# First tokens and taps loaded first, statistics ahead of the taps' product, and two steps of the step-size chain moved to VectorE

## The chip, the core and the metric

The kernel runs on one core of one Trainium2 chip. The core has five engines that take their instructions in order, each from its own list: TensorE (PE in the profile), VectorE (DVE), ScalarE (ACT), GpSimd (POOL) and SyncE (SP), which here issues the loads and stores. They meet only through semaphores. The metric is the device time of one execution, in microseconds, as the median of several.

## The reference, cut to what matters

Two layers, each a mixer and a feed-forward part, every part on a layer norm of the running sum, over 2048 tokens of 128 features. The change lies in the first part, a selective scan:

```python
xz = x @ in_proj_w                       # 128 -> 512, split into x_in and z
x_in, z = jnp.split(xz, 2, axis=-1)
xc = silu(causal_conv(x_in, conv_w, 4 taps) + conv_b)
ssm_out = xc @ x_proj_w                  # B (16), C (16) and one column for dt
dt = softplus(ssm_out[..., -1:] @ dt_w + dt_b)
A = -jnp.exp(A_log)
y = _selective_scan(xc, dt, A, B_p, C_p, D_param)
return y * silu(z) @ out_proj_w
```

The scan needs exp(dt * A) and dt * B * xc for 16 states of 256 channels. After it come a mixture of 8 experts and a shared one, an attention with 16 heads whose queries and keys pass convolutions, and a second mixture with a choice of 2 of 8 experts.

## The kernel before, in words

The tokens are taken in four chunks of 512. The scan part runs over `k` = 0 to 63, 16 states for each chunk, and each `k` has two halves `g` of 128 channels. `scan_order` (line 77) is an order written out by hand that each engine's program goes through with its own functions: first `start()`, then for each `k` the steps `rows`, `scanP`, `mulW`, `mulB`, `scanX`, `mulC`, `clamp` and `sums`, with the next chunk's `prolog` and the last chunk's `epilog` and feed-forward pulled in between piece by piece. `attention_order` is the like for what follows.

The change touches the start, chunk 0. SyncE issues all loads in one queue: `x_tok` (all 2048 tokens, 1 MB, semaphore `d_x`), then nine loads under one semaphore `d_scan`, the input projection `w_in` and the convolution's taps `w_cv` ahead of seven small ones down to `w_out`, then the feed-forward weights (`d_ffn`) and the attention's (`d_att`); after these it goes into `start()` (line 2169), where it writes the rows B and C to `bc` in HBM, and then issues the row loads of `rows(k)`.

VectorE multiplies the taps into `w_in` (line 1389), so that convolution and projection are one product on TensorE, copies `starts` into bank 2 of PSUM (line 1392), and takes the statistics of chunk 0 in `norm` (lines 1397 and 1401). GpSimd's `power` (from line 1879) makes the inverse deviation and the shift. ScalarE normalizes (line 1111), TensorE transposes (line 615), ScalarE copies back (line 1117), and TensorE does the tap products (line 626) into banks 7 and 6, the gate products (line 630) and, behind ScalarE's two Silus (line 1121), the row product (line 634) and the step-size products (line 638).

The step size is softplus(v) = max(v, 0) + log(1 + exp(-|v|)), the logarithm by three quartics: ScalarE does |v| (line 1132), the exponential (line 1134), the positive part (line 1135) into `vv2`, and pairs of squares (lines 1143 and 1147, the second written to the bank that held v); VectorE multiplies the three factors (line 1412) and adds the positive part (line 1417) to give `DL[0]`. GpSimd multiplies this with the convolved input `U[0]` into `DU[0]` (line 1906). ScalarE's `rows(0)` makes exp(dt * A) (line 1206), GpSimd's `clamp` (line 1942) bounds it, and `mulB` (line 1926) multiplies `DU` with B. Then VectorE's scans follow (lines 1449, 1455, 1463).

Of the kernel before, what the change touches and what calls it, by code (L numbers as in the profile page):

```python
# [6 lines left out]
ALU = mybir.AluOpType  # L7
ACT = mybir.ActivationFunctionType
# [58 lines left out]
def drain(gen):  # L67
    for _ in gen or ():
        pass
# [328 lines left out]
def build(nc, A, out):  # L398
    with ExitStack() as ctx:
        S = Signals(nc, ctx)  # L400
# [6 lines left out]
        def bank(i):  # L407
            return PS[:, i, :]

        x_tok = sb("x_tok", [128, NB, 128])  # L410
# [3 lines left out]
        cst = sb("cst", [128, 6])  # L414
# [32 lines left out]
        with ExitStack() as ph:  # L447
# [3 lines left out]
            w_in = D2[:, 6144:6656]  # L451
# [5 lines left out]
            w_db = sa("w_db", [128, 2])  # L457
# [114 lines left out]
            w.wait_ge(S("end"), 5)  # L572


        X_IN, W_SCAN, W_FFN, W_ATT = 16, 16 * 9, 16 * 12, 16 * 14
        KEY_ROWS = 16 * 18
        W_EXPERTS = 16 * 35

# [524 lines left out]
        def scalar_program(e):  # L1103
# [10 lines left out]
            def start():  # L1114
                scaled(0, 0, xn1, 0, "p")
                w.wait_ge(S("p_tp"), 1)
                e.activation(XN[:, 0:C], bank(7), ACT.Copy).then_inc(S("p_ln"), 1)
                w.wait_ge(S("d_scan"), W_SCAN)
                for g in range(2):
                    w.wait_ge(S("p_mm_x"), g + 1)  # L1120
# [9 lines left out]
                for g in range(2):  # L1130
                    w.wait_ge(S("p_mm_dt"), g + 1)
                    e.activation(yy2[g], bank(7 - g), ACT.Abs, bias=w_db[:, g:g + 1]).then_inc(S("s_abs"), 1)
                    w.wait_ge(S("s_abs"), g + 1)
                    e.activation(yy2[g], yy2[g], ACT.Exp, scale=-1.0).then_inc(S("s_exp"), 1)
                    e.activation(vv2[g], bank(7 - g), ACT.Relu, bias=w_db[:, g:g + 1]).then_inc(S("s_vv"), 1)
                for r in range(3):
                    for g in range(2):
                        n = 4 * r + 2 * g
# [245 lines left out]
        def vector_program(e):  # L1384
            w = Waits(e)
            e.memset(xnT[:, 0:1], 0.0).then_inc(S("edge"), 1)
            e.memset(xnT[:, T + 1:T + 2], 0.0).then_inc(S("edge"), 1)
            w.wait_ge(S("d_scan"), W_SCAN)
            e.tensor_tensor(w_cv[:, :, :], w_cv[:, :, :], w_in[:, 0:256].unsqueeze(1).to_broadcast([128, 4, 256]),
                            ALU.mult).then_inc(S("taps"), 1)  # L1390
            w.wait_ge(S("const"), 11)
            e.tensor_copy(bank(2), starts[:, :]).then_inc(S("starts"), 1)

            def norm(i, tc, st, pre, pause=2):

# [6 lines left out]
                yield from idle(pause + 2)  # L1402

            def start():
                w.wait_ge(S("d_x"), X_IN)
                drain(norm(0, 0, 0, "p"))
                for r, (_, _, more) in enumerate(QUARTICS):
                    for g in range(2):
                        if r:
                            w.wait_ge(S("s_pp"), 2 * r + g - 1)  # L1410
                        w.wait_ge(S("s_sq"), 4 * r + 2 * g + 2)
                        e.scalar_tensor_tensor(out=pp2[g], in0=bank(7 - g), scalar=more, in1=pp2[g] if r else yy2[g],
                                               op0=ALU.add, op1=ALU.mult).then_inc(S("s_pp"), 1)
                for g in range(2):
                    w.wait_ge(S("s_pp"), 5 + g)
                    w.wait_ge(S("s_vv"), g + 1)
                    e.scalar_tensor_tensor(out=DL[0][:, g, :], in0=pp2[g], scalar=LEAD, in1=vv2[g], op0=ALU.mult,
                                           op1=ALU.add).then_inc(S("p_dl"), 1)

            def prolog(tc):  # L1420
                Dx = DL[tc % 2]
                yield from norm(tc, tc, 4 * (tc % 2), "p")
                yield from idle(11)
                for g in range(2):
# [440 lines left out]
        def gpsimd_program(e):  # L1865
# [30 lines left out]
            def start():  # L1896
                power(0, 0, "p")
                for x in range(8):
                    e.memset(rank[:, :, x], 8.0 - x).then_inc(S("tables"), 1)
                w.wait_ge(S("d_scan"), W_SCAN)  # L1900
                for g in range(2):
                    e.tensor_scalar(skip[:, g, :], ident[:, :], w_D[:, g:g + 1], None, ALU.mult).then_inc(S("tables"), 1)
                for g in range(2):
                    w.wait_ge(S("p_dl"), g + 1)
                    w.wait_ge(S("p_u"), g + 1)
                    e.tensor_tensor(DU[0][:, g, :], DL[0][:, g, :], U[0][:, g, :], ALU.mult).then_inc(S("p_du"), 1)

            def prolog(tc):
                yield
                power(tc, 4 * (tc % 2), "p")  # L1910
# [220 lines left out]

        def sync_program(e):
            w = Waits(e)
            e.dma_start(x_tok[:, :, :], A["L0_attn_x"].rearrange("o (b p) d -> p (o b) d", p=128)).then_inc(S("d_x"), 16)
            e.dma_start(w_in[:, :], A["L0_attn_in_proj_w"]).then_inc(S("d_scan"), 16)
            e.dma_start(w_cv[:, :, :], A["conv_taps"].partition_broadcast(128)).then_inc(S("d_scan"), 16)
            e.dma_start(w_cb[:, :], A["L0_attn_conv_b"]).then_inc(S("d_scan"), 16)
            e.dma_start(w_xp[:, :, :], A["L0_attn_x_proj_w"].rearrange("(g p) n -> p g n", p=128)).then_inc(
                S("d_scan"), 16)
# [1 line left out]
            e.dma_start(w_db[:, :], A["L0_attn_dt_b"]).then_inc(S("d_scan"), 16)  # L2141
            e.dma_start(w_al[:, :, :], A["L0_attn_A_log"].rearrange("(g p) n -> p g n", p=128)).then_inc(
                S("d_scan"), 16)
            e.dma_start(w_D[:, :], A["L0_attn_D_param"]).then_inc(S("d_scan"), 16)
            e.dma_start(w_out[:, :, :], A["L0_attn_out_proj_w"].rearrange("(g p) n -> p g n", p=128)).then_inc(
                S("d_scan"), 16)
# [246 lines left out]
```

## Time and profile before

| what | value |
|---|---|
| times of three runs, us | 1527.34, 1530.22, 1535.51 (median 1530.22) |
| profiled execution: span of its instructions, us | 1529.1 |
| profiled execution: its own time | not listed apart from the three |
| busy share of the span | TensorE 85%, VectorE 79%, ScalarE 69%, GpSimd 44% |
| busy before 54 us | TensorE 15.43, VectorE 10.41, ScalarE 25.03, GpSimd 10.62 |
| mean granted TensorE clock, of full speed | 0.932 |

The profile is of one execution. Its starts are counted from the first instruction. "Idle before, releaser" is the time for which an engine had nothing to run ahead of a group, and what ended that. A line's number is that of the code above. The KB column of the DMA view shows 0.5 for `x_tok`, the size of one of its pieces; the whole is 1 MB.

### The profile page before, as it was taken

The numbers are of one execution on the slowest core, as the hardware profiler recorded it, in microseconds if no ns is written. First come the engines' busy times: TensorE is split into PE (matmuls) and PEld (weight loads), VectorE is DVE, ScalarE is ACT, GpSimd is POOL, SyncE is SP. The second block draws the span as 40 slices with busy tenths as digits, with TensorE's granted clock in tenths as the row PEclk, the third lists the DMA queues.
The fourth block names the chain that finished last, engine by engine and source line by source line (L and its number), as shares of the span: only waits on it lengthen the run. The fifth ranks groups of instructions, "written<-read, shape, count | busy, mean of one in ns | idle before, by whom it ended". The sixth has DMA issues, their size and how long they took to land.

```text
span 1529.1 us, 22573 instructions
## 1 busy us (share of the span) xinstructions
PE 1305.2 (85%) x8424; PEld 506.3 (33%) x8424; DVE 1206.0 (79%) x1435; ACT 1058.4 (69%) x1839; POOL 668.8 (44%) x652
## 2 busy tenths in 40 slices
PE   4364689988977997886499999999999998999998
PEld 1121234333443443332122222222222222236963
DVE  0799988898989871776699999999999997933522
ACT  3552379768837825453179998999899987997643
POOL 1688868977978856661403112111111123111430
PEclk9677789999988998997689999999999998999999
DMA  8221222223323202421213001100010000010210
GB/s 220 66 82 70 76 66 88 90 70 83 96 70 84 82 21 55 88 43 37 41 35 51 30 30 48 23 2 2 2 23 2 2 2 19 6 29 12 74 32 28
DMA packets 63696, 75.71 MB, mean 50 GB/s; under 512 B 8633, under 2 KB 39226, under 8 KB 63458
## 3 DMA queue, kind: packets, MB, share of 16 engines
q1 hardware_dynamic: 62818, 72.70, 17.9%
q0 software_dynamic: 768, 1.57, 0.3%
q8 instruction: 66, 1.08, 0.3%
q14 instruction: 44, 0.36, 0.1%
HBM read 66.04 MB, written 8.21 MB: 49 GB/s over the span
## 4 chain that ended last, share of the span: by engine, by line
PE 52%; DVE 26%; ACT 9%; issue 7%; POOL 4%; DMA 1%; SPq 1%; another core or an unknown queue 0%; DVEq 0%; POOLq 0%; ACTq 0%
DVE mx L1670 16%; PE PS L980 11%; PE PS L968 6%; PE PS L736 5%; PE PS L745 5%; PE PS L937 4%; PE PS L688 2%; PE PS L1052 2%; PE PS L1067 2%; DVE D L1463 2%; DVE PS L1449 2%; PE PS L1088 2%; PE PS L1076 2%; ACT D L1206 1%; POOL D L1926 1%
## 5 line engine op out<-in xcount | busy, mean ns | idle before, releaser
L1343 ACT ACTIVATE aa<-PS 128x512 f32<-128x512 f32 x1024 | 551.7, 598 | 63.0 <-PE PS L968 51.4
L1670 DVE TENSOR_REDUCE mx<-PS 128x2 f32<-128x1024 f32 x480 | 552.8, 1215 | 15.6 <-PE PS L937 7.3
L980 PE MATMUL PS<-aa,D 128*32 128x256 f32 x4096 | 322.9, 393 | 1.5 <-ACT aa L1343 0.6
L968 PE MATMUL PS<-D 54*128 54x512 bf16 x1024 | 213.1, 391 | 13.0 <-ACT aa L1343 8.3
L2044 POOL CAST n<-nm 4x512 bf16<-4x512 f32 x15 | 9.0, 602 | 453.7 <-ACT nm L1325 453.7
L937 PE MATMUL PS<-D 51*128 51x512 bf16 x960 | 191.3, 386 | 17.2 <-DVE mx L1670 16.6
L1449 DVE TENSOR_TENSOR_SCAN PS<-PS,D 128x512 f32<-128x512 f32 x128 | 157.5, 1231 | 11.1 <-POOL D L1942 3.5
L745 PE MATMUL PS<-xnT,f_w 128*128 128x512 f32 x288 | 158.3, 644 | 6.1 <-ACT HB L1233 5.5
L1233 ACT ACTIVATE HB<-PS 128x512 f32<-128x512 f32 x144 | 84.1, 595 | 104.7 <-PE PS L745 98.4
L736 PE MATMUL PS<-HB,f_w 128*128 128x512 f32 x288 | 146.3, 618 | 6.1 <-DVE GO L1537 5.9
L980 PEld LDWEIGHTS PS<-aa,D 128*32 128x32 f32 x4096 | 84.3, 108 | 192.8 <-issue 154.3
L1206 ACT ACTIVATE D<-D,Am 128x512 f32<-128x512 f32 x128 | 85.1, 713 | 75.7 <-DVE D L1463 73.7
L688 PE MATMUL PS<-D,ident 128*128 128x512 f32 x192 | 107.5, 685 | 32.9 <-POOL D L1933 28.1
L1933 POOL TENSOR_TENSOR D<-D 128x1024 f32<-128x1024 f32 x48 | 112.9, 2353 | 48.5 <-DVE D L1463 48.3
L968 PEld LDWEIGHTS PS<-D 54*128 54x128 bf16 x1024 | 53.4, 93 | 225.3 <-ACT aa L1343 160.1
L1463 DVE TENSOR_TENSOR_SCAN D<-D,hl,PS 128x512 f32<-128x512 f32 x96 | 122.6, 1277 | 2.9
L1926 POOL TENSOR_TENSOR D<-D 128x1024 f32<-128x1024 f32 x48 | 112.8, 2350 | 3.3
L736 PEld LDWEIGHTS PS<-HB,f_w 128*128 128x128 f32 x288 | 57.0, 200 | 82.8 <-issue 70.5
L745 PEld LDWEIGHTS PS<-xnT,f_w 128*128 128x128 f32 x288 | 53.9, 200 | 73.3 <-issue 51.6
L688 PEld LDWEIGHTS PS<-D,ident 128*128 128x128 f32 x192 | 39.4, 213 | 90.6 <-issue 50.9
L1455 DVE SCALAR_TENSOR_TENSOR PS<-PS,D 128x512 f32<-128x512 f32 x96 | 66.8, 696 | 2.8 <-POOL D L1926 0.5
L1942 POOL TENSOR_SCALAR D<-D 128x1024 f32<-128x1024 f32 x64 | 66.5, 1040 | 5.5
(333 smaller groups left out, 1700.2 us busy)
## 6 DMA issues: line engine op xcount, KB each, us to landing
D<-bc SPq DMA_DIRECT2D x128, 256.0 KB, 3.5
GB<-gd SPq DMA_DIRECT2D x32, 256.0 KB, 3.7
D<-sc SPq DMA_DIRECT2D x72, 64.0 KB
aa<-in_L_ffn_W SPq DMA_DIRECT2D x9, 256.0 KB, 3.2
D<-in_L_ffn_W SPq DMA_DIRECT2D x9, 256.0 KB, 3.6
f_w<-in_L_ffn_experts_w SPq DMA_DIRECT2D x1, 2048.0 KB, 9.2
f_w<-in_L_ffn_experts_w SPq DMA_DIRECT2D x8, 256.0 KB, 5.9
aa<-gh SPq DMA_DIRECT2D x1, 2048.0 KB, 8.3
```

The source lines that it names most:

```text
L688: e.matmul(bank(g), ident[:, :], wb[k % 4][:, g, :], start=(n == 0), stop=(n == 15)).then_inc(S("mm_sum"), 1)
L736: e.matmul(down_bank(tc, n // 4), f_w2[:, n // 4, n % 4, :], HB1[i % 6], start=(n % 4 == 0), stop=(n % 4 == 3)).then_inc(S("mm_down"), 1)
L745: e.matmul(bank(4 + i % 2), f_w1[:, n // 4, 128 * (n % 4):128 * (n % 4) + 128], XN[:, ts], start=True, stop=True).then_inc(S("mm_up"), 1)
L937: t = e.matmul(to[:, hh, :], query(hh, qc % 2, p, b), KS[64 * hh:64 * hh + 51, p, 512 * c:512 * c + 512], start=True, stop=True)
L968: e.matmul(take_exp(s + hh), KS[64 * hh:64 * hh + 54, p, 128 * kb:128 * kb + 128], QP[64 * hh:64 * hh + 54, qc % 2, p, :], start=True, sto ...
L980: t = e.matmul(PS[32 * j:32 * j + 32, 7, cs], va[:, kb, 9 * h:9 * h + 32], Pt[K % 3][:, 512 * j + 256 * n:512 * j + 256 * n + 256], start= ...
L1343: e.activation(Pt[K % 3][:, c:c + 512], bank((s + hh) % 3), ACT.Exp).then_inc(S("e_free"), 1)
L1449: e.tensor_tensor_scan(out=bank(3), data0=bank(2), data1=ab[k % 3][:, g, :], initial=0.0, op0=ALU.max, op1=ALU.mult).then_inc(S("sP"), 1)
L1463: e.tensor_tensor_scan(out=pb[k % 2][:, g, :], data0=ab[k % 3][:, g, :], data1=bank(3), initial=hl[:, 16 * g + n:16 * g + n + 1] if tc els ...
L1670: e.tensor_reduce(mx4[:, G % 2, b, 2 * pair:2 * pair + 2, c:c + 1], max_banks(m), AX.X, ALU.max).then_inc(freed(m)[0], 1)
L1926: e.tensor_tensor(wb[k % 4], DU[tc % 2][:, :, :], Bb[k % 3].unsqueeze(1).to_broadcast([128, 2, C]), ALU.mult).then_inc(S("wB"), 1)
L1933: e.tensor_tensor(wb[k % 4], pb[k % 2], Cb[k % 3].unsqueeze(1).to_broadcast([128, 2, C]), ALU.mult).then_inc(S("xC"), 1)
```

## The change

Five edits, all at the start of the kernel.

1. SyncE loads the first four of the 16 token blocks first (256 KB, semaphore `d_x0`), then `w_in` and the taps under a semaphore of their own (`d_taps`), then five small loads, then the other twelve token blocks (`d_x`), then `w_D` and `w_out`. `d_scan` now counts seven loads. VectorE's `prolog` waits for `d_x` before its statistics.
2. VectorE takes the statistics of chunk 0 first, and multiplies the taps and copies `starts` after them.
3. ScalarE runs one Silu over one column of constants, into a place of `Am` that is written again later, after it has copied the transposed tokens back.
4. The positive part of chunk 0 is one VectorE instruction for each half, add and then maximum, and waits for ScalarE's |v| of that half.
5. `DU[0]` is made by VectorE, after `DL[0]`, and no longer by GpSimd.

```diff
@@ -572,7 +572,7 @@
             w.wait_ge(S("end"), 5)
 
 
-        X_IN, W_SCAN, W_FFN, W_ATT = 16, 16 * 9, 16 * 12, 16 * 14
+        X_IN, W_TAPS, W_SCAN, W_FFN, W_ATT = 16, 16 * 2, 16 * 7, 16 * 12, 16 * 14
         KEY_ROWS = 16 * 18
         W_EXPERTS = 16 * 35
 
@@ -1115,6 +1115,8 @@
                 scaled(0, 0, xn1, 0, "p")
                 w.wait_ge(S("p_tp"), 1)
                 e.activation(XN[:, 0:C], bank(7), ACT.Copy).then_inc(S("p_ln"), 1)
+                w.wait_ge(S("const"), 8)
+                e.activation(Am[:, 0:1], cst[:, 0:1], ACT.Silu)
                 w.wait_ge(S("d_scan"), W_SCAN)
                 for g in range(2):
                     w.wait_ge(S("p_mm_x"), g + 1)
@@ -1132,7 +1134,6 @@
                     e.activation(yy2[g], bank(7 - g), ACT.Abs, bias=w_db[:, g:g + 1]).then_inc(S("s_abs"), 1)
                     w.wait_ge(S("s_abs"), g + 1)
                     e.activation(yy2[g], yy2[g], ACT.Exp, scale=-1.0).then_inc(S("s_exp"), 1)
-                    e.activation(vv2[g], bank(7 - g), ACT.Relu, bias=w_db[:, g:g + 1]).then_inc(S("s_vv"), 1)
                 for r in range(3):
                     for g in range(2):
                         n = 4 * r + 2 * g
@@ -1385,11 +1386,6 @@
             w = Waits(e)
             e.memset(xnT[:, 0:1], 0.0).then_inc(S("edge"), 1)
             e.memset(xnT[:, T + 1:T + 2], 0.0).then_inc(S("edge"), 1)
-            w.wait_ge(S("d_scan"), W_SCAN)
-            e.tensor_tensor(w_cv[:, :, :], w_cv[:, :, :], w_in[:, 0:256].unsqueeze(1).to_broadcast([128, 4, 256]),
-                            ALU.mult).then_inc(S("taps"), 1)
-            w.wait_ge(S("const"), 11)
-            e.tensor_copy(bank(2), starts[:, :]).then_inc(S("starts"), 1)
 
             def norm(i, tc, st, pre, pause=2):
 
@@ -1402,8 +1398,17 @@
                 yield from idle(pause + 2)
 
             def start():
-                w.wait_ge(S("d_x"), X_IN)
+                w.wait_ge(S("d_x0"), X_IN)
                 drain(norm(0, 0, 0, "p"))
+                w.wait_ge(S("d_taps"), W_TAPS)
+                e.tensor_tensor(w_cv[:, :, :], w_cv[:, :, :], w_in[:, 0:256].unsqueeze(1).to_broadcast([128, 4, 256]),
+                                ALU.mult).then_inc(S("taps"), 1)
+                w.wait_ge(S("const"), 11)
+                e.tensor_copy(bank(2), starts[:, :]).then_inc(S("starts"), 1)
+                w.wait_ge(S("d_scan"), W_SCAN)
+                for g in range(2):
+                    w.wait_ge(S("s_abs"), g + 1)
+                    e.tensor_scalar(vv2[g], bank(7 - g), w_db[:, g:g + 1], 0.0, ALU.add, ALU.max).then_inc(S("s_vv"), 1)
                 for r, (_, _, more) in enumerate(QUARTICS):
                     for g in range(2):
                         if r:
@@ -1416,9 +1421,14 @@
                     w.wait_ge(S("s_vv"), g + 1)
                     e.scalar_tensor_tensor(out=DL[0][:, g, :], in0=pp2[g], scalar=LEAD, in1=vv2[g], op0=ALU.mult,
                                            op1=ALU.add).then_inc(S("p_dl"), 1)
+                for g in range(2):
+                    w.wait_ge(S("p_dl"), g + 1)
+                    w.wait_ge(S("p_u"), g + 1)
+                    e.tensor_tensor(DU[0][:, g, :], DL[0][:, g, :], U[0][:, g, :], ALU.mult).then_inc(S("p_du"), 1)
 
             def prolog(tc):
                 Dx = DL[tc % 2]
+                w.wait_ge(S("d_x"), X_IN)
                 yield from norm(tc, tc, 4 * (tc % 2), "p")
                 yield from idle(11)
                 for g in range(2):
@@ -1900,11 +1910,6 @@
                 w.wait_ge(S("d_scan"), W_SCAN)
                 for g in range(2):
                     e.tensor_scalar(skip[:, g, :], ident[:, :], w_D[:, g:g + 1], None, ALU.mult).then_inc(S("tables"), 1)
-                for g in range(2):
-                    w.wait_ge(S("p_dl"), g + 1)
-                    w.wait_ge(S("p_u"), g + 1)
-                    e.tensor_tensor(DU[0][:, g, :], DL[0][:, g, :], U[0][:, g, :], ALU.mult).then_inc(S("p_du"), 1)
-
             def prolog(tc):
                 yield
                 power(tc, 4 * (tc % 2), "p")
@@ -2131,9 +2136,10 @@
 
         def sync_program(e):
             w = Waits(e)
-            e.dma_start(x_tok[:, :, :], A["L0_attn_x"].rearrange("o (b p) d -> p (o b) d", p=128)).then_inc(S("d_x"), 16)
-            e.dma_start(w_in[:, :], A["L0_attn_in_proj_w"]).then_inc(S("d_scan"), 16)
-            e.dma_start(w_cv[:, :, :], A["conv_taps"].partition_broadcast(128)).then_inc(S("d_scan"), 16)
+            tokens = A["L0_attn_x"].rearrange("o (b p) d -> p (o b) d", p=128)
+            e.dma_start(x_tok[:, 0:4, :], tokens[:, 0:4, :]).then_inc(S("d_x0"), 16)
+            e.dma_start(w_in[:, :], A["L0_attn_in_proj_w"]).then_inc(S("d_taps"), 16)
+            e.dma_start(w_cv[:, :, :], A["conv_taps"].partition_broadcast(128)).then_inc(S("d_taps"), 16)
             e.dma_start(w_cb[:, :], A["L0_attn_conv_b"]).then_inc(S("d_scan"), 16)
             e.dma_start(w_xp[:, :, :], A["L0_attn_x_proj_w"].rearrange("(g p) n -> p g n", p=128)).then_inc(
                 S("d_scan"), 16)
@@ -2141,6 +2147,7 @@
             e.dma_start(w_db[:, :], A["L0_attn_dt_b"]).then_inc(S("d_scan"), 16)
             e.dma_start(w_al[:, :, :], A["L0_attn_A_log"].rearrange("(g p) n -> p g n", p=128)).then_inc(
                 S("d_scan"), 16)
+            e.dma_start(x_tok[:, 4:16, :], tokens[:, 4:16, :]).then_inc(S("d_x"), 16)
             e.dma_start(w_D[:, :], A["L0_attn_D_param"]).then_inc(S("d_scan"), 16)
             e.dma_start(w_out[:, :, :], A["L0_attn_out_proj_w"].rearrange("(g p) n -> p g n", p=128)).then_inc(
                 S("d_scan"), 16)
```

## Rows read from the trace of the kernel before

**Rows 1.** The chain that ended last: shares of the span by engine (page).

```profile
PE 52%; DVE 26%; ACT 9%; issue 7%; POOL 4%; DMA 1%; SPq 1%; another core or an unknown queue 0%; DVEq 0%; POOLq 0%; ACTq 0%
```

**Rows 2.** Windows; columns: TensorE, weight load, VectorE, ScalarE, GpSimd, granted clock, DMA share, GB/s.

```profile
0.00:54.00 54.00, 15.43 (x32) 6.10 (x32) 10.41 (x25) 25.03 (x39) 10.62 (x33) 0.84 0.63 178
54.00:86.00 32.00, 20.44 (x43) 8.13 (x44) 30.37 (x33) 15.88 (x23) 28.84 (x23) 0.79 0.16 52
...
162.00:1000.00 838.00, 723.04 (x3620) 276.70 (x3620) 704.38 (x872) 568.96 (x886) 467.19 (x446) 0.93 0.23 59
```

**Rows 3.** Waits, 0 to 45 us: total, times, longest.

```profile
DVE D L1389 <- DMA w_out<-in_L_attn_out_proj_w: 10.1, 1, 10.1
```

**Rows 4.** Timeline, 0 to 20 us; columns: start, us, engine, line, what.

```profile
0.86 0.88 SPq L2134 DMA_DIRECT2D x_tok<-in_L_attn_x  x1
...
11.08 1.23 DVE L1389 TENSOR_TENSOR D<-D 128x1024 f32<-128x1024 f32 x1 [10.11 <-DMA w_out<-in_L_attn_out_proj_w]
...
12.81 0.86 DVE L1397 BATCH_NORM_STATS2 st<-x_tok 128x6 f32<-128x128 f32 x4
...
19.85 8.81 PE L626 MATMUL PS<-xnT,D 128*128 128x512 f32 x16 [0.78 <-ACT xnT L1117]
```

**Rows 5.** DMA issues, of the start and then whole span: KB, us to landing.

```profile
x_tok<-in_L_attn_x SPq DMA_DIRECT2D x1, 0.5 KB, 6.5
...
D<-bc SPq DMA_DIRECT2D x128, 256.0 KB, 3.5
```

**Rows 6.** Line 2183 (row loads of B), 30 to 60 us.

```profile
L2183 SPq DMA_DIRECT2D D<-bc x4: 320/381/433, 34.5 to 54.4; - x4
...
DMA to landing us min/median/max: 3.4/4.6/5.5
```

**Rows 7.** Timeline, weight loads of the tap passes.

```profile
22.55 0.34 PEld L626 LDWEIGHTS PS<-xnT,D 128*128 128x128 f32 x1 [0.52 <-issue]
...
23.37 0.19 PEld L626 LDWEIGHTS PS<-xnT,D 128*128 128x128 f32 x1 [0.48 <-issue]
23.80 0.19 PEld L626 LDWEIGHTS PS<-xnT,D 128*128 128x128 f32 x1 [0.24 <-issue]
```

**Rows 8.** Timeline of ScalarE, 25 to 39 us.

```profile
25.32 1.28 ACT L1121 ACT_TABLE_LOAD   x1 [5.62 <-PE PS L626]
...
28.70 0.69 ACT L1121 ACTIVATE U<-PS,w_cb 128x512 f32<-128x512 f32 x1 [1.39 <-PE PS L626]
...
35.78 0.67 ACT L1135 ACTIVATE D<-PS,w_db 128x512 f32<-128x512 f32 x1
36.35 0.68 ACT L1132 ACTIVATE GO<-PS,w_db 128x512 f32<-128x512 f32 x1
...
37.60 0.67 ACT L1135 ACTIVATE FO<-PS,w_db 128x512 f32<-128x512 f32 x1
38.17 0.71 ACT L1143 ACTIVATE SQ<-D,cst 128x512 f32<-128x512 f32 x1
```

**Rows 9.** Timeline, 28 to 52 us (a narrower window gives fewer of a group).

```profile
28.65 0.44 SPq L2167 DMA_DIRECT2D bb<-in_L_attn_out_b  x1
...
32.87 0.33 SPq L2171 DMA_DIRECT2D bc<-D  x1
...
47.74 0.68 DVE L1417 SCALAR_TENSOR_TENSOR D<-GO,FO 128x512 f32<-128x512 f32 x1
47.91 2.86 POOL L1906 TENSOR_TENSOR D<-D,U 128x512 f32<-128x512 f32 x2 [30.32 <-DVE D L1417]
...
47.91 1.64 POOL L1906 TENSOR_TENSOR D<-D,U 128x512 f32<-128x512 f32 x1 [30.32 <-DVE D L1417]
47.92 1.95 ACT L1206 ACTIVATE D<-D,Am 128x512 f32<-128x512 f32 x3 [1.49 <-DVE D L1417]
...
50.86 1.04 POOL L1942 TENSOR_SCALAR D<-D 128x1024 f32<-128x1024 f32 x1
```

**Rows 10.** VectorE's groups by line and form: busy us, mean ns.

```profile
L1854 DVE TENSOR_TENSOR aa<-aa 128x512 f32<-128x512 f32 x7 | 4.8, 691 | 0.2
```

## What the change does to the time: the prediction

> **What bounds the kernel now.** I read the chain that ended last first: its largest shares are TensorE (52%) and VectorE (26%) [rows 1]. Those are averages over stages with different limits, so next come the windows by stage [rows 2]. The reader is to see that in the first 54 us no engine is busy for half of the time: this stretch is a string of waits, one engine at a time. From 54 to 86 us VectorE is busy 30.4 of 32 us and GpSimd 28.8, and from 162 to 1000 us TensorE and VectorE share the load at a granted clock of 0.93. The change touches only the first 54 us. Everything behind it depends on what the start hands over (the first step sizes), nothing behind it waits for a fixed hour, and so whatever is taken off this string should arrive at the end, if the later stages run as before.
>
> The string, step by step. VectorE does nothing until 11.08, and the wait view names the last of the nine loads that it counts, the one of w_out [rows 3]. Then it multiplies the taps (1.23 us), copies `starts`, and only at 12.81 begins the statistics of the first tokens, whose load had landed 6.5 us after its issue at 0.86, at 7.4 [rows 4, 5]. From the statistics over GpSimd's power, ScalarE's normalization, transposes and copy to the first tap product on TensorE (19.85) it is 7.04 us [rows 4]. Then come products and activations, the quartics' squares from 38.17 [rows 8], the second step size at 47.74, GpSimd's two products of step size and input, its clamp at 50.86, and the scan [rows 9].
>
> **The start of the loads and the order on VectorE.** This is the largest term. Statistics now wait for 256 KB of tokens alone. The trace has no such load at the start; the nearest row is a load of the same 256 KB over a quiet queue, 3.5 us at the median [rows 5]. From above the bound is the 6.5 us that the 1 MB took, from below the 3.4 us of the fastest row load of that size in the start [rows 6]. I take 3.5, because the size is the same and the queue empty: the tokens are there at 0.86 + 3.5 = 4.36. Nothing stands ahead of the statistics on VectorE now but two tiny memsets. With the 7.04 us of before, the tap products could begin at 4.36 + 7.04 = 11.40 instead of 19.85: **8.45 us earlier**.
>
> They also need the taps' product. Its two loads (256 and 512 KB) stand behind the 256 KB of tokens, together the 1 MB that x_tok was before, so I expect them at about 7.4; three issues instead of one cost the queue some tenths (0.88 us for the large one [rows 4]), and their packets are no smaller. The product then ends at 7.4 + 1.23 = 8.6, well ahead of 11.40, and the copy of `starts` behind it too (it is wanted only by the scan). If the taps came as late as the last load does now, the product would end at 12.3 and the gain would be 7.5 instead of 8.45. The remaining 12 of the 16 token blocks land near 9 to 10 us; their reader is the next prolog, which begins its statistics only after 52 us, so the new wait for `d_x` there is free. The seven loads left under `d_scan` stay ahead of the large weights and land near 11 us as now, plus at most one issue; their first reader is the first Silu, at about 25.3 - 8.45 = 16.9. GpSimd's two `skip` products behind the same wait are done long before its clamp.
>
> SyncE's queue is what could spoil this, since a later step of the start issues from it. The write of the B and C rows waits for ScalarE's copy, and goes out at 32.87 now; SyncE is done with the weights at 28.65 + 0.44 = 29.1 [rows 9]. Shifted by 8.45 the copy would be ready at 24.4, so now the write waits for the queue until 29.1 and gains only 3.8 us. But its reader is not near: row loads land 3.4 to 5.5 us after their issue, which is 34.5 for the first [rows 6]. Even if it landed as late as today, at 40.0 at most, the first product that reads it would be wanted near 41. The queue hides this, with 1 us to spare in the worst case and 5 us in the likely one.
>
> **The Silu that loads its table early.** The table load of 1.28 us stands between the first tap product and the first Silu [rows 8]. It moves beside the tap products, at no cost, as ScalarE is idle there for 5.62 us [rows 8]. I count **no gain** for it: the second Silu waits again for TensorE, 1.39 us [rows 8], and TensorE works without a break through the gate products to the row product, which wants both. Bounds: 0 to 1.3 us.
>
> **The positive part on VectorE.** ScalarE loses two Relus, each 0.57 us from its start to the next instruction's (35.78 to 36.35 for the first, and the second stands likewise ahead of the square at 38.17) [rows 8]: 2 x 0.57 = **1.14 us**, on the path, since ScalarE has no idle time between them and the square. On VectorE, idle there, each costs some 0.69 us, between the end of the Abs that it now waits for and the first square written to the same bank; the tighter one starts at the second Abs's end and has two squares of slack. Without that cover it would cost up to 0.69. Queued behind its wait are only VectorE's quartic steps, which come after these squares anyway.
>
> **The first product of step size and input on VectorE.** GpSimd needs 2.86 us for the two, and its clamp waits for that until 50.86 [rows 9]. On VectorE a product of this form takes 0.691 us [rows 10]; behind the second step size (ends at 48.42) the two end near 49.7. The clamp then needs only ScalarE's two first decays: three take 1.95 us from 47.92, so two are there at about 49.25. Gain 50.86 - 49.25 = 1.6. But GpSimd's first product took 1.64 us while VectorE's last step size (two inputs in SBUF) ran beside it, the second 2.86 - 1.64 = 1.22 alone [rows 9]: 0.4 us of hindrance. The clamp would begin under VectorE's second product, which also reads two SBUF tensors, and I charge it the same 0.4: **1.2 us**, bounds 0.8 and 1.6. From there VectorE's scans follow as before. The Trainium skill ("GPSIMD Engine Reference", its table of the engine) says the same of this edit, and it speaks against it: GpSimd's SBUF interface is shared with VectorE and contended by VectorE instructions that read two SBUF inputs. Without the rule the sum would have 1.6 here, by it no more than 1.2; the trace agrees with it, by those 0.4 us. The taps' product can now run beside GpSimd's small power steps (5.8 to 7.9); the same effect could hold them for up to 1.2 us. I take nothing, as the taps land about when the last of them runs, and keep it in the range.
>
> **Sum.** 8.45 + 0 + 1.14 + 1.2 = 10.8 us. The profiled execution had a span of 1529.1 us, 1.1 below the median of the times (1530.2), and that I take for what lies around it. Span after: 1518.3. Time after: **1519.4 us**, 0.7% less.
>
> **The rivals.** (1) *The first tokens do not land first.* Packets of the three first loads share 16 engines; if they interleave, the tokens land only when the whole 1 MB has, at 7.4. For it: the 1 MB itself took 6.5 us. Against it: loads of 256 KB issued close together, the row loads of the start, still landed in 3.4 to 5.5 us [rows 6], and the tokens are issued first. Products at 7.4 + 7.04 = 14.4, first term 5.4 instead of 8.45, time 1522.4. Chance 12%.
>
> (2) *TensorE starts cold and stays so for longer.* The weight loads of the first tap passes come 0.82 us apart, from 23.37 on 0.43 [rows 7]: the engine went from its 1.2 GHz level to its 2.4 GHz level after the transposes and some four tap passes from 19.85 on, though the profile's column says 1.00 for this stretch. 28 passes lie on the path up to the step-size product, and about four were slow. If half of the other 24 stay slow in the new place (a pause before the taps would do that), that is 12 x 0.43 = 5 us: time 1524.4; if all do, 1529.7. Against it: the string of transposes, copy and products keeps its spacing. Chance 10%.
>
> (3) *The later stages run at a lower clock; this ends slower.* From 162 to 1000 us the mean clock is 0.93 [rows 2], so 2 x 0.07 x 838 = 117 us are already at 1.2 GHz, in a stretch where TensorE is busy 86% of the time. A start that comes 11 us sooner changes when its pauses fall. From the point where 22 us more are at half rate (a mean of 0.917), the gain of 10.8 is gone; at a mean of 0.90 it is 50 us more and up to 25 us lost, 1544 us. For it: nothing but this dependence on timing, and the three times of before, which differ by 8 us without any change. Against it: engines stay in step by the same waits, so the same pauses should recur. Chance 10%, half of it above 1538. The Trainium skill ("TensorE: Matmul & The Clock Gate", Part 1) calls the point at which the clock rises variable from run to run; no row here shows two runs of this.
>
> **How the numbers follow.** Forecast 68%, rivals 12, 10 and 10. The likeliest case's own range is 1515 to 1523: 1.6 us below for a faster load and no hindrance, and some 3 us of scatter on either side. The range that should hold 8 in 10 reaches down to 1513 and up to 1526, which takes in rival 1 and the half of rival 2, and leaves out the rest and rival 3. This kernel's measurement tells 0.5% (7.6 us) from no change, so faster means under 1522.6. Of the forecast's 68, 64 are below that, of rival 1's 12 half, of rivals 2 and 3 one each: 72% faster. Slower: 5%. The same: 23%.
>
> **What would show it.** Right: statistics of the first tokens begin at 4 to 5 us, ahead of the taps' product; first tap pass at 11 to 12; Silu's table load inside the tap products, with the gate products' end 8 to 9 us sooner; four ScalarE instructions between the last table load's users and the first square instead of six; clamp at 40 to 40.5 (50.86 - 10.8), near 1.1 us long or longer; first scan near 41. The stage windows behind it, moved by 11 us, should show the same busy times and the clock of 0.93. Wrong: statistics after 7 us (rival 1), more than six tap passes at 0.85 us (rival 2), a clock under 0.92 between 150 and 990 us (rival 3), or a first row load that lands after the clamp and holds the product.

## The result and the profile after

| | us |
|---|---|
| changed kernel, four runs | 1520.36, 1521.57, 1522.66, 1524.80 (median 1522.12) |
| kernel before, four runs | 1527.34, 1530.22, 1534.88, 1535.51 (median 1532.55) |
| ratio | 0.994, 95% interval 0.9924 to 0.9956 |
| profiled execution: time, span, mean granted clock | 1522.66, 1520.9, 0.921 |

The change takes 0.6% off, with 0.4 to 0.8% as the interval: the kernel is faster, and only the lower end of the interval is under the 0.5% that the prediction asked for. The forecast was 1519.4 with 1513 to 1526 as the range. Between medians the gain is 10.4 us where 10.8 were forecast; between the two profiled spans it is only 8.2.

First the start of the timeline, for the order of the loads and of VectorE (columns: start, us, engine, line, what).

```profile
0.80 0.43 SPq L2140 DMA_DIRECT2D x_tok<-in_L_attn_x  x1
...
3.69 0.87 DVE L1393 BATCH_NORM_STATS2 st<-x_tok 128x6 f32<-128x128 f32 x4 [2.73 <-DMA x_tok<-in_L_attn_x]
...
6.84 0.20 POOL L1903 TENSOR_TENSOR shift<-shift,rstd 128x4 f32<-128x4 f32 x1
...
7.37 1.23 DVE L1404 TENSOR_TENSOR D<-D 128x1024 f32<-128x1024 f32 x1 [2.39 <-DMA D<-in_conv_taps]
...
10.61 1.28 ACT L1119 ACT_TABLE_LOAD   x1
...
10.74 9.27 PE L626 MATMUL PS<-xnT,D 128*128 128x512 f32 x16 [0.78 <-ACT xnT L1117]
...
20.05 0.69 ACT L1123 ACTIVATE U<-PS,w_cb 128x512 f32<-128x512 f32 x1 [2.67 <-PE PS L626]
```

Statistics begin at 3.69 (12.81 before), the taps' product at 7.37, the first tap pass at 10.74 (19.85) [rows 4]. From statistics to tap pass it is 7.05 us, 7.04 before. Next the end of the start, for the three moved operations.

```profile
26.69 0.75 DVE L1411 TENSOR_SCALAR D<-PS,w_db 128x512 f32<-128x512 f32 x1 [17.49 <-ACT D L1134]
...
27.84 0.75 DVE L1411 TENSOR_SCALAR FO<-PS,w_db 128x512 f32<-128x512 f32 x1 [0.40 <-ACT GO L1134]
...
28.37 0.70 ACT L1144 ACTIVATE SQ<-D,cst 128x512 f32<-128x512 f32 x1
...
30.12 0.43 SPq L2178 DMA_DIRECT2D bc<-D  x1
...
33.34 0.32 SPq L2190 DMA_DIRECT2D D<-bc  x1
...
37.94 0.69 DVE L1422 SCALAR_TENSOR_TENSOR D<-GO,FO 128x512 f32<-128x512 f32 x1
...
38.54 1.29 DVE L1427 TENSOR_TENSOR D<-D,U 128x512 f32<-128x512 f32 x2
39.54 1.19 POOL L1947 TENSOR_SCALAR D<-D 128x1024 f32<-128x1024 f32 x1 [26.62 <-ACT D L1207]
40.76 1.23 DVE L1459 TENSOR_TENSOR_SCAN PS<-PS,D 128x512 f32<-128x512 f32 x1 [0.93 <-POOL D L1947]
```

The first square starts 9.80 us sooner than before, the second step size 9.80, the clamp 11.32 [rows 8, 9], and the first scan 11.18 (it began at 51.94). So the start gave more than the sum said. By the end of the span 8.2 are left. The stage windows do not show where the rest goes: from 162 us on TensorE and VectorE are busy for the same time as before within 0.4% [rows 2], ScalarE for 1% more and GpSimd for 2% less, at a clock of 0.92 and not 0.93.

```profile
0.00:54.00 54.00, 17.64 (x37) 7.47 (x38) 23.58 (x44) 28.23 (x46) 18.44 (x41) 0.77 0.67 191
...
162.00:1000.00 838.00, 725.86 (x3680) 276.71 (x3684) 703.55 (x865) 574.61 (x898) 458.44 (x438) 0.92 0.22 58
```

I laid the starts of VectorE's 128 scans of the first kind (those of line 1449 before, 1459 after) side by side. The changed kernel leads by 11.18 us at the first, by 9.75 from the thirteenth on (94.89 against 85.14), by 10.60 at the 67th, by 5.02 at the 83rd, and by 6.65 at the last (550.64 against 543.99). A new wait would take its share once and keep it; here the lead falls and rises again. The first fall can be read off one wait. VectorE stood idle for ScalarE's first square of the second chunk for 1.6 us before and for 3.0 us now, because the tap products that this square waits for took longer. Both kernels' rows, before:

```profile
64.53 5.26 PE L654 MATMUL PS<-xnT,D 128*128 128x512 f32 x8 [0.69 <-ACT xnT L1156]
```

and after:

```profile
53.36 6.74 PE L654 MATMUL PS<-xnT,D 128*128 128x512 f32 x8 [0.69 <-ACT xnT L1157]
```

The same eight passes, no wait among them: 6.74 us is eight at the half rate, 5.26 is about four at half and four at full rate (the eight passes of this line that follow, all at the full rate, take 3.60 in both). The largest fall, 2.8 us between the 71st and the 72nd scan, can be read off as well:

```profile
313.73 0.69 DVE L1490 TENSOR_TENSOR x_tok<-x_tok,PS 128x512 f32<-128x512 f32 x1 [2.70 <-PE PS L701]
```

VectorE waited 2.70 us for TensorE's products of line 701. Eight tap passes ahead of them (line 654) had taken 5.85 us; the kernel before does them in 3.70 and has no such wait.

### The profile page after: what moved, and what is told of

Read it like the earlier page. It is cut to its first block, busy times and chain, and to the rows that moved or that the text cites. A ratio compares the mean times of both kernels' runs of the same rounds, so it can differ in the third digit from the quotient of the medians.

```text
span 1520.9 us, 22574 instructions
## 1 busy us (share of the span) xinstructions
PE 1308.2 (86%) x8424; PEld 506.1 (33%) x8424; DVE 1210.3 (80%) x1439; ACT 1057.7 (70%) x1838; POOL 665.7 (44%) x650
## 4 chain that ended last, share of the span: by engine, by line
PE 50%; DVE 23%; POOL 9%; issue 8%; ACT 8%; DMA 2%; SPq 1%; another core or an unknown queue 0%; POOLq 0%; DVEq 0%; ACTq 0%
DVE mx L1680 15%; PE PS L980 12%; PE PS L968 6%; PE PS L745 5%; PE PS L736 5%; PE PS L937 4%; POOL D L1931 3%; PE PS L1052 2%; PE PS L1067 2%; PE PS L688 2%; PE PS L1088 2%; PE PS L1076 2%; POOL D L1947 2%; DVE D L1473 1%; PE PS L654 1%
```

## The experiments

**Theory A:** the start gives what its parts say, it arrives at the end in full, and what varies is how long TensorE runs at its 1.2 GHz level in the later stages. **Theory B:** the change brings in a new wait behind the first scan.

**The changed kernel once more, twelve runs.** No edit.

> The changed kernel once more, for its scatter. Theory A (the start gave 11 us, and up to 3 of them go lost or not by TensorE's clock in the scan and feed-forward stages): the first scan begins again at 40.8 us within 0.1, while the span differs from run to run by some us, and the runs with the higher mean clock are the shorter ones; about 1.5 to 2.5 us of span for 0.005 of clock. Theory B (the loss behind the first scan is a new wait that the change brings in, a row load or a full engine): every run ends 1520 to 1521, with no relation to the clock, and the shift against before falls at the same places.

Measured: median 1520.32 against 1529.59, ratio 0.995 (0.9934 to 0.9966). The first scan is at 41.26, and not within 0.1 of 40.8: the 16 tap passes took 9.77 us this time and not 9.27. The twelve runs fall into two groups: six with a mean clock of 0.930 or 0.931 have spans of 1515.5 to 1518.2 (mean 1516.7), six with 0.916 to 0.922 have 1519.0 to 1525.0 (mean 1522.6). The kernel before, on the same chip, had 0.926 to 0.933 in all of its 18 runs, and 1526.9 as the mean of the 13 at 0.929 or more. Between the runs of 0.929 and more the gain is 1526.9 - 1516.7 = 10.2 us.

The profile of this run is one of the first group: span 1516.2, clock 0.931. Set beside the kernel before (1529.1, 0.932), its scans lead by 10.68 us at the first and by 10.57 at the 128th, and by 10.57 to 10.70 everywhere between. The same program in the first profile led by 4.92 to 11.18. Theory B falls: a new wait of the program would be in both. VectorE's addition to `x_tok` of above, which waited 2.70 us for line 701, waits for nothing here, and the eight tap passes ahead took 3.70 us:

```profile
310.04 0.67 DVE L1490 TENSOR_TENSOR x_tok<-x_tok,PS 128x512 f32<-128x512 f32 x1
```

The windows of the two profiles of one and the same program, the longer one first:

```profile
86.00:151.00 65.00, 34.16 (x38) 10.74 (x39) 62.66 (x65) 17.84 (x27) 57.73 (x41) 0.53 0.22 73
...
300.00:450.00 150.00, 133.12 (x347) 60.86 (x345) 132.27 (x163) 103.04 (x137) 117.32 (x84) 0.91 0.26 75
```

```profile
86.00:151.00 65.00, 34.79 (x39) 11.17 (x40) 62.70 (x64) 16.89 (x26) 57.65 (x42) 0.68 0.24 75
...
300.00:450.00 150.00, 130.70 (x345) 60.50 (x343) 135.84 (x176) 101.65 (x136) 120.07 (x86) 0.94 0.25 78
```

From 86 to 151 us the clock 0.53 instead of 0.68 costs nothing (VectorE is busy 62.7 of 65 us in both). From 300 to 450 us 0.91 instead of 0.94 does: TensorE is busy longer, and VectorE gets less done.

**The loads and VectorE's order alone.** The kernel before with the first two of the five edits. Their main lines, cut (the taps' own semaphore, the second load of tokens and the copy of `starts` are as in the change):

```diff
-            e.dma_start(x_tok[:, :, :], ...).then_inc(S("d_x"), 16)
+            e.dma_start(x_tok[:, 0:4, :], tokens[:, 0:4, :]).then_inc(S("d_x0"), 16)
...
+                w.wait_ge(S("d_x0"), X_IN)
+                drain(norm(0, 0, 0, "p"))
+                w.wait_ge(S("d_taps"), W_TAPS)
+                e.tensor_tensor(w_cv[:, :, :], ...).then_inc(S("taps"), 1)
```

> The kernel before plus the loads' order, the split of x_tok and the order on VectorE; the early Silu, the Relus and the first product of step size and input as before. By the sum: first tap pass at 10.74 as in the changed kernel, first scan 8.65 sooner than 51.94, at 43.3; the time 8.7 us under before if all of it arrives at the end, 6 to 11 with the clock's scatter. A rival in which the other three edits carry the gain has the first scan at 48 or later.

Measured: 1519.5 against 1529.59, ratio 0.9932 (0.991 to 0.9955); first scan at 44.96, not 43.3. One us of the difference is a thing that I had named and taken at nothing. Its rows:

```profile
6.80 1.22 DVE L1403 TENSOR_TENSOR D<-D 128x1024 f32<-128x1024 f32 x1 [1.83 <-DMA D<-in_conv_taps]
6.84 1.25 POOL L1894 TENSOR_TENSOR shift<-shift,rstd 128x4 f32<-128x4 f32 x1
```

The taps landed at 6.80. GpSimd's last step, four numbers for each partition, then takes 1.25 us where it took 0.20 in the changed kernel's profile: it ends when VectorE's product of two SBUF tensors ends. ScalarE's normalization starts at 8.12, not 7.08. The other 0.6 us are TensorE's: the tap products took 9.90 us here, 9.27 there. The loads and the order carry most of the gain, 7.0 of 11.2 us at the first scan; in the time the other three edits made no difference that these runs can tell.

**VectorE's order undone.** The changed kernel, with the taps' product and the copy of `starts` put back ahead of the statistics.

> The changed kernel with the order on VectorE alone undone: the taps' product and the copy of starts stand ahead of the first statistics, the loads stay as changed. By the sum: statistics begin when the taps have landed (6.8 to 7.4) plus 1.8 us, near 9.0 instead of 3.7, so the first scan comes 5.2 us later, at 46 to 46.5, and the time 5 us over the changed kernel's. If only the loads' order mattered, the first scan would stay at 41 to 42.

Measured: 1519.88 against 1522.84, ratio 0.9978 (0.9965 to 0.9991). This is another chip, on which the changed kernel itself was not run, so its time can be set beside this one only by the ratios (0.995 on the first chip, 0.28% less, some 4 us; 5 were expected). Statistics at 8.26 and not 3.69, first tap pass at 15.30, 4.56 us later; first scan at 44.64, 3.9 us later only, because TensorE happened to be quicker (tap products in 8.59 us). That is less than the 5.2 us expected for the scan. The taps' product could start at 6.52 here, sooner than I had reckoned. The loads without the order bring the first tap pass from 19.85 to 15.30, half of the 9.1 us.

**The first load whole.** The changed kernel, with all 16 token blocks loaded first (and so without the `prolog`'s wait for `d_x`).

```diff
-            e.dma_start(x_tok[:, 0:4, :], tokens[:, 0:4, :]).then_inc(S("d_x0"), 16)
+            e.dma_start(x_tok[:, :, :], tokens).then_inc(S("d_x0"), 16)
...
-            e.dma_start(x_tok[:, 4:16, :], tokens[:, 4:16, :]).then_inc(S("d_x"), 16)
```

> The changed kernel with all 16 token blocks in the first load, as before, and all else as changed. By the sum: the 1 MB lands at 7.4, so statistics begin then and not at 3.7, and the taps, 768 KB behind it, near 9.5 to 10, with the product done by 11.3; first tap pass at 7.4 + 7.05 = 14.45, 3.7 us after that of the changed kernel, first scan at 44.5 to 45. If the order of the loads carried nothing, first scan at 41.

Measured: 1524.41 against 1529.76, ratio 0.9959 (0.9939 to 0.9979). Statistics at 7.28, the taps' product at 9.51, first tap pass at 14.48, first scan at 43.80. The first three are as expected; the scan came a little sooner, as the tap products took 8.57 us. GpSimd's last step was held again: it began at 10.43, inside VectorE's product (9.51 to 10.73), and took 0.36 us. The step ahead of it had begun at 9.31, before that product, and took its usual 1.04 us. The order without the split brings the first tap pass to 14.48, 5.4 of the 9.1 us; splitting the load adds the last 3.7. In this run and in the one before, the taps keep a semaphore of their own; that part of the change was not tested alone. An estimate from these rows: with the 1 MB load first the taps' product can start at 9.51, and statistics behind it begin 1.74 us later (6.52 to 8.26 in the run before this one), which makes 11.25 where the kernel before has 12.81: some 1.6 us.

**The early Silu undone.**

```diff
-                w.wait_ge(S("const"), 8)
-                e.activation(Am[:, 0:1], cst[:, 0:1], ACT.Silu)
```

> The changed kernel without the early Silu: the table load goes back between the first tap product and the first Silu. By the prediction nothing changes behind the second Silu, which again waits for TensorE: first scan 40.8 to 41.3, as in the changed kernel. A rival in which the load was on the path has the first scan 1.3 us later, at 42.1 to 42.6.

Measured: 1514.17 against 1522.84, ratio 0.9944 (0.9931 to 0.9957); first scan at 41.06. ScalarE's rows:

```profile
16.97 1.28 ACT L1121 ACT_TABLE_LOAD   x1 [6.53 <-PE PS L626]
18.27 0.69 ACT L1121 ACTIVATE U<-PS,w_cb 128x512 f32<-128x512 f32 x1
20.35 0.69 ACT L1121 ACTIVATE U<-PS,w_cb 128x512 f32<-128x512 f32 x1 [1.39 <-PE PS L626]
```

The table load is back in front of the first Silu, and the second waits for TensorE all the same, 1.39 us (2.67 with the early load). Worth nothing, as forecast.

**The positive part back on ScalarE.** The Relu of line 1135 back, VectorE's add and maximum out.

> The changed kernel with the positive part back on ScalarE. By the sum the first square starts 1.15 us later after the first |v|, 3.62 and not 2.47, and the first scan with it, near 42. Theory A on the clock (the start's phase decides how many tap and up products meet the lower clock) says that this small shift may also change how often runs fall near a clock of 0.92: 6 of 12 for the changed kernel, 0 of 18 for the one before. Theory B (an instruction of the change causes the low clock) says it stays at about half.

Measured: 1516.96 against 1522.84, ratio 0.9961 (0.9946 to 0.9976). The times of this kernel do not tell 1.1 us apart, but the profile does: from the first |v| (25.48) to the first square (29.10) 3.62 us, 2.47 in the changed kernel (25.90 to 28.37).

**The product of step size and input back on GpSimd.** Lines 1903 to 1906 back, VectorE's out.

> The changed kernel with the first product of step size and input back on GpSimd. By the sum the clamp waits for it, and the first scan comes 11.18 - 8.65 - 1.15 = 1.4 us later against the second step size (4.20 us after its start and not 2.82), at 42.2. On the clock as in the run with the positive part back on ScalarE: if a shift of the start by 1.4 us changes how often the clock is near 0.92, it is the phase and not an instruction.

Measured: 1518.65 against 1522.84, ratio 0.9969 (0.9957 to 0.9981). From the second step size to the first scan 4.20 us (37.52 to 41.72), 2.82 in the changed kernel: 1.38 us. The clamp's 1.04 us are 1.19 in the changed kernel, where it begins beside VectorE's second product: held by 0.15.

**Constant products on TensorE, ahead of the first transposes only, and ahead of the second chunk's too.** Nobody reads their results; the second kernel has both edits, the first only the first.

```diff
+                w.wait_ge(S("const"), 11)
+                for _ in range(4):
+                    e.matmul(bank(0), ident[:, :], starts[:, :], start=True, stop=True)
...
+                if tc == 1:
+                    w.wait_ge(S("p_st"), 16)
+                    for _ in range(6):
+                        e.matmul(bank(4), ident[:, :], starts[:, :], start=True, stop=True)
```

> The changed kernel plus the four products of constants ahead of the first transposes alone. Theory A: first scan at 38.7 (5 passes by 0.43 us), second chunk's first tap passes still slow, 5.3 to 6.8 us, as TensorE again idles for 25 us before them; time 2 us under the changed kernel, within its scatter. Theory B: the same start, and the same places of loss behind it.

> The changed kernel plus products of constants on TensorE whose results nobody reads: four ahead of the first transposes and six ahead of the second chunk's transposes, where it stands idle for 7 and 25 us. Theory A: the five tap passes of the start that were 0.85 us apart run at 0.43, first scan 2 us sooner (38.7), and the second chunk's first eight tap passes take 3.6 us and not 6.7, so the wait of VectorE for the second chunk's first square (3.0 us) goes away; together 3 to 5 us less than the changed kernel, about 1517.5. Theory B: the start gains 2 us, but nothing is gained at the second chunk. Against both: the products delay the transposes, no gain.

Measured: 1517.47 and 1517.38, beside 1520.32 for the changed kernel and 1529.59 for the one before, ratios 0.9935 (0.9915 to 0.9956) and 0.9928 (0.9906 to 0.995). First scans at 38.06 and 38.07. TensorE's rows of the kernel with both:

```profile
2.50 5.51 PE L621 MATMUL PS<-starts,ident 128*128 128x512 f32 x8 [2.50 <-POOL starts L1893]
8.79 0.66 PE L615 MATMUL PS<-ident,xn 128*128 128x128 f32 x4 [0.78 <-ACT xn L1117]
10.23 7.08 PE L628 MATMUL PS<-xnT,D 128*128 128x512 f32 x16 [0.78 <-ACT xnT L1123]
...
50.88 3.70 PE L660 MATMUL PS<-xnT,D 128*128 128x512 f32 x8 [0.69 <-ACT xnT L1163]
```

The 16 tap passes take 7.08 us instead of 9.27, and the second chunk's eight 3.70 instead of 6.74 (5.28 with the first edit alone). VectorE's wait for the second chunk's first square falls from 3.0 us to 0.2. So it was the clock: four products of constants ahead of the transposes change nothing else that these passes need. That the second edit then does not show in the time is within the scatter of five and six runs.

**Both, and the taps' product kept off GpSimd's last step.**

```diff
                 w.wait_ge(S("d_taps"), W_TAPS)
+                w.wait_ge(S("p_shift"), 1)
```

> The changed kernel with both sets of constant products on TensorE (as in the earlier run with both) and one more wait: the taps' product starts only after GpSimd's last step for the shift. In the run with the loads alone this step took 1.25 us instead of 0.20 because the taps had landed 0.04 us before it began; with the wait ScalarE's normalization starts at 6.8 to 7.1 in every run, and the taps' product, wanted at 10.2, ends at 8.4. First scan 38.0; time 10 to 14 us under the kernel before and 2 to 4 under the changed one, runs within 5 us of each other but for the clock.

Measured: 1518.5 against 1529.76, ratio 0.9924 (0.9906 to 0.9943), 11.3 us under the kernel before. First scan at 38.09, GpSimd's step 0.20 us. The added wait is not what did that here: the taps landed at 7.20, after the step had ended (6.99), so the wait held nothing and stays untested. The kernel beats the one before clearly. Against the changed kernel it leads by 2.7 us in the first scan; their ratios' intervals (0.9924 here, 0.995 and 0.994 there) overlap a little, and so do its runs (clocks 0.920 to 0.935): two of the six fell to 0.923 or less.

**The kernel before, with its start put off.** Four and five more copies of `starts` on VectorE ahead of the statistics, and nothing of the change.

> The kernel before, with four more copies of starts one after the other on VectorE, which only put off the first statistics, by 4 x 0.7 = 2.8 us. Theory A (where the start ends decides how often the clock of the later stages is near 0.92): the first scan is at 54.7, which lies against the start of the changed kernel as another place against TensorE's clock does; some runs of this kernel, perhaps half, then show a clock of 0.925 or less, and are 5 to 6 us longer than the others, though no instruction of the change is in it. Theory B (the change's own instructions do it): all runs stay at 0.929 to 0.934 like those of the kernel before, and the time is 2.8 us over it.

> The kernel before with five such copies, first scan 3.5 us later. Theory A: the share of runs with a clock of 0.925 or less differs from that of the run with four copies, and may be none at all. Theory B: none, time 3.5 us over the kernel before. If both delayed kernels never show the lower clock, the place of the start does not explain it and its cause stays open.

Measured: 1533.7 and 1534.8 against 1529.76, ratios 1.0026 (1.0012 to 1.004) and 1.0034 (1.002 to 1.0047), first scans at 55.22 and 55.49. A start that ends 3.3 and 3.6 us later ends the kernel 3.9 and 5.0 us later: what the start takes does arrive. On how often the clock is at 0.925 or less they say little: one run of 12, three of 12, and three of 26 of the kernel before beside them. Theory A had half of the runs with four copies. Over all runs the share was 3 of 62 for the kernel before, 9 of 16 for the changed one, 7 of 12 without the order, 4 of 9 with the whole load, 3 of 6 without the early Silu, 2 of 6 with the Relus back, 0 of 6 with GpSimd's product back, 0 of 4 with the loads alone, 6 of 17 for the three with constant products. The change makes it more frequent; what in it does is open.

The mark of 0.925 misses part of it. The scans of all the profiles, laid beside those of the kernel before like the first ones, show the lead in us (a minus is a lag):

| profile | clock | first scan | 83rd | 128th |
|---|---|---|---|---|
| changed kernel, once more | 0.931 | 10.68 | 10.60 | 10.57 |
| without the early Silu | 0.934 | 10.88 | 10.86 | 10.84 |
| constant products at the start | 0.931 | 13.88 | 13.82 | 13.80 |
| both constant products and the wait | 0.933 | 13.85 | 15.23 | 15.08 |
| changed kernel, first profile | 0.921 | 11.18 | 5.02 | 6.65 |
| both constant products | 0.924 | 13.87 | 10.57 | 12.20 |
| loads and order alone | 0.928 | 6.98 | 3.69 | 5.29 |
| without the order | 0.924 | 7.30 | 1.73 | 1.59 |
| the whole load | 0.921 | 8.14 | 2.56 | 2.43 |
| Relus back | 0.925 | 10.45 | 5.39 | 5.31 |
| GpSimd's product back | 0.926 | 10.22 | 5.44 | 5.41 |
| four copies more | 0.926 | -3.28 | -3.64 | -3.76 |
| five copies more | 0.925 | -3.55 | -9.38 | -7.77 |

Of the eleven profiles with an earlier start four kept their lead, seven lost part of it, among them the two whose shares are 0 of 6 and 0 of 4. So those shares acquit none of the edits. The kernel before with five copies lost 6 us in the same place without any instruction of the change. And the losses come in patterns that repeat: from the thirteenth scan on, the first profile of the changed kernel and that of the kernel with both constant products are 5.51 to 5.56 us apart at every scan, though one has the lower clock's long passes in the second chunk and the other does not; the changed kernel's second profile is 10.57 to 10.70 us from the kernel before. Which pattern an execution takes is not settled by the program alone: the changed kernel had both.

## Why the prediction was right, and where it was not

- **The largest term.** Forecast 8.45 us, from tokens landing 3.5 us after their issue. They took 2.9 (issue at 0.80, statistics at 3.69), so the first tap pass came 9.11 us sooner, of which TensorE gave back 0.46, its tap products taking 9.27 us and not 8.81. Mis-sized by 0.2 in sum; the 7.04 us from statistics to tap pass (7.05), and the taps at 7.4 (7.37), were right. The term holds by 8.65 us at the end of the tap passes. Rival 1, tokens no sooner than the rest, did not happen.
- **The table load.** Forecast nothing, shown to be nothing by undoing it.
- **The positive part.** 1.14 forecast, 1.15 measured (3.62 to 2.47), shown by undoing it. VectorE's 0.75 us lies in the cover, as said.
- **The first product on VectorE.** 1.2 forecast, 1.38 measured. The hindrance was there and smaller, 0.15 us and not 0.4, as the overlap was shorter. The Trainium skill's rule ("GPSIMD Engine Reference", table of the engine), that GpSimd's SBUF interface is contended by VectorE instructions with two SBUF inputs, agrees: 0.15 us at the clamp, 1.05 at the last step for the shift, each begun while such a VectorE instruction ran.
- **What I took at nothing there** was not always nothing. "As the taps land about when the last of them runs" was true, and which comes first changed: at 7.37 they were late enough, at 6.80 they cost 1.05 us, which I had bounded at 1.2.
- **SyncE's queue.** The write of the rows went out at 30.12, 29.1 forecast, as the queue was done with the weights only at 30.07, and then took 3.2 us instead of 1.6, so the first row load was issued at 33.34. With the longest landing of the first three B loads (6.1 us) it is there at 39.4, ahead of the first product at 40.81: it hid the loss, but with 1.4 us to spare and not the 5 that I called likely.
- **The sum.** 10.8 forecast up to the clamp and the scan, 11.2 measured; at the end 10.2 between the runs of 0.929 and more, 10.4 between the first medians, 9.3 between the medians of the 12 and 18 later runs. That 10.4 lies so near 10.8 is in part luck: three of the changed kernel's first four runs had a clock of 0.925 or less, and the kernel before had its highest median of all in its first four. The gain arrives in full where the later stages keep the pattern of the kernel before (10.68 us at the first scan and 10.57 at the last of the first kind); in other executions 2 to 6 us of it go lost by then. The forecast's "if the later stages run as before" was the condition that mattered. The 1.1 us taken for what lies around the span are 1.7 to 1.8 in each run; this drops out of the time, which is the earlier median less the sum.
- **Rivals 2 and 3, the clock.** Both mechanisms are real here, and neither turned the sign. TensorE's slow passes cost 2.2 us at the start (9.27 against 7.08) and were there before as well; rival 2's 5 us more did not come. Rival 3's lower clock came in half of the changed kernel's runs: 6 us longer between the two groups. I gave it 10% as the case that decides the sign; it decides between 4 and 10 us of gain instead. I had priced it too high: half a us lost for each us at the half rate. The groups' mean clocks are 0.012 apart, by the working of rival 3 some 36 us more at the half rate (an estimate), and they differ by 6 us, a sixth and not half: much of that time costs nothing, as between 86 and 151 us above. That the clock makes the 6 us is read off two waits and the correlation of clock and span over the 12 runs (-0.95); no run held the later stages at the full rate. My argument against it, that the same waits bring the same pauses, was wrong as a forecast: the same program, run twice, had other stretches at the half rate.

## What to carry to other kernels

At the start of a kernel the first consumer's data should be a load of its own ahead of all else, and each engine's first instruction should be the one whose data lands first; each without the other gave 4.6 and 5.4 of 9.1 us, with a semaphore for the taps alone in both. Price such a change in the profile, by the time of the first instruction of the steady stage, because the time of the whole moves by more than the gain with TensorE's clock; then compare runs of like mean clock, and judge an edit's effect on the clock by where its trace loses time and not by a mark set on the mean. When a step on VectorE moves to another time, look at what GpSimd begins in that moment, however small: 0.2 us can become 1.25.

## What the runs showed that I had not expected

- A product of two SBUF tensors on VectorE held a GpSimd instruction on four columns that began 0.04 us after it, from 0.20 to 1.25 us, to its own end. A GpSimd instruction that had begun before such a product (9.31 against 9.51, the whole load) was not held.
- One program had mean granted clocks from 0.916 to 0.931 on one chip, and 1515.5 to 1525.0 us of span with them. The changed kernel was at 0.925 or less in 9 of 16 runs, the kernel before in 3 of 62. The cause is open. The Trainium skill ("TensorE: Matmul & The Clock Gate", Part 1) calls the point at which the clock rises variable from run to run; these runs agree: the 16 tap passes of the start took 9.27 and 9.77 us in two executions of the changed kernel.
- Four constant products while TensorE has nothing to do made the tap products 2.2 us shorter and the first scan 2.7 us sooner. The granted clock's column shows 1.00 for that stretch either way; the passes' own distance (0.85 or 0.43 us) shows the level.
